# Attention and feed-forward block: x, attention's result and the output laid out by pairs and blocks of tiles in DRAM

## What is computed

```python
# cross attention: every query row sees 4 neighbouring rows of a table of 154 keys and values
q = split_heads(layernorm(x) @ Wq.T)                       # 16 heads of 32
k, v = split(ctx @ Wkv.T)
scores = einsum(q, k[seg_id - 0..3]) * 32 ** -0.5          # masked where the index is below 0
x = x + (softmax(scores) @ v[seg_id - 0..3]) @ Wo.T
# gated feed-forward, with every intermediate quantised to int16 by its own global peak
h = act_qdq(layernorm(x))
up, gate = act_qdq(h @ up_w.T), act_qdq(h @ gate_w.T)      # 4-bit weights, 1536 columns
gate = act_qdq(gate * fixed_qdq(sigmoid(gate)))
x = x + act_qdq(gate * up) @ down_w.T
```

## Time and profile before

| what | value |
|---|---|
| median of three runs | 2336.34 us |
| profiled execution, its own time | 2335.28 us |
| its span in the trace | 2333.4 us |
| PE, DVE, ACT, POOL busy | 87%, 76%, 58%, 29% of the span |
| DMA | 132025 packets, 637.74 MB, 273 GB/s |
| attention with its start and its drain | 0 to 642 us |
| products for gate and up | 646 to 1643 us |
| stretch without matmuls | 1643 to 1824 us |
| product for down, last stores | 1824 to 2333 us |

### The profile page before, as it was taken

How to read it: one execution, slowest core, us unless ns; L and a number is a source line. 1 busy time by engine, 2 the same in 40 slices (tenths; PEclk the granted TensorE clock), 3 DMA queues, 4 the chain that set the end, 5 groups by cost and what they waited for, 6 DMA issues and landing times.

```text
span 2333.4 us, 25335 instructions
## 1 busy us (share of the span) xinstructions
PE 2019.0 (87%) x9524; PEld 944.9 (40%) x9524; DVE 1766.4 (76%) x1404; ACT 1349.1 (58%) x1571; POOL 667.4 (29%) x664
## 2 busy tenths in 40 slices
PE   5888888888599999999999999999100799999998
PEld 2444444444344444444444444444000344444443
DVE  8799999999746756665599999999699744457541
ACT  4678788887422322222399886766699633446430
POOL 2599999999300000000011101222010000000000
PEclk9999999999899999999999999999655899999999
DMA  7789999998346755753699986886899855555641
GB/s 297 278 316 336 353 331 349 338 343 334 126 158 234 243 216 196 250 180 134 236 406 416 413 341 251 292 320 253 355 418 372 317 224 216 208 204 217 234 153 72
DMA packets 132025, 637.74 MB, mean 273 GB/s; under 512 B 12352, under 2 KB 12864, under 8 KB 91968
## 3 DMA queue, kind: packets, MB, share of 16 engines
q1 hardware_dynamic: 86464, 318.91, 37.4%
q0 software_dynamic: 45440, 317.21, 34.8%
HBM read 431.73 MB, written 204.34 MB: 273 GB/s over the span
## 4 chain that ended last, share of the span: by engine, by line
PE 64%; issue 2%; ACT 2%; DVE 2%; DMA 1%; POOL 0%; DVEq 0%; ACTq 0%; POOLq 0%
PE fd_pp L1810 43%; PE fd_pp L1824 21%; ACT ff_ring L1753 1%; DMA ff_ring<-gate_integers 1%; DVE ff_sig L1609 1%; DMA kept_gate<-gate_integers 0%; DVE ff_h_parts L1593 0%; ACT kept_gate L1757 0%; DVE ff_sq L1529 0%; ACT ff_gin L1757 0%; DVE ff_sq L1600 0%; ACT ff_hq L1757 0%; POOL ff_o_all L898 0%; ACT ff_sig L1740 0%; ACT ff_ring L1779 0%
## 5 line engine op out<-in xcount | busy, mean ns | idle before, releaser
L1824 PE MATMUL fd_pp<-ff_down,kept_gate 128*128 128x512 f16 x1536 | 458.3, 380 | 181.4 <-DVE ff_up L1650 181.4
L1810 PE MATMUL fd_pp<-ff_h_parts,kept_gate 128*128 128x512 f16 x2304 | 499.4, 380 | 14.2 <-DVE ff_h_parts L1421 14.2
L1810 PE MATMUL fd_pp<-ff_h_parts,ff_up 128*128 128x512 f16 x2304 | 497.4, 379 | 0.0
L1673 ACT ACTIVATE ff_raw<-fd_pp 128x1024 f32<-128x1024 f32 x192 | 195.1, 1020 | 399.5 <-PE fd_pp L1810 394.4
L1810 PEld LDWEIGHTS fd_pp<-ff_h_parts,kept_gate 128*128 128x128 f16 x2304 | 225.8, 98 | 287.7 <-DVE ff_h_parts L1421 14.6
L1810 PEld LDWEIGHTS fd_pp<-ff_h_parts,ff_up 128*128 128x128 f16 x2304 | 225.4, 98 | 271.9
L1824 PEld LDWEIGHTS fd_pp<-ff_down,kept_gate 128*128 128x128 f16 x1536 | 150.5, 98 | 363.7 <-issue 183.3
L1824 PE MATMUL fd_pp<-ff_down,ff_up 128*128 128x512 f16 x768 | 291.7, 380 | 0.0
L1437 DVE TENSOR_REDUCE ff_gate_top<-ff_raw 128x1 f32<-128x2048 f32 (+1 forms) x49 | 109.8, 2242 | 187.2 <-ACT ff_raw L1673 187.2
L1779 ACT ACTIVATE ff_ring<-ff_hq,kept_g 128x2048 int16<-128x2048 f32 x48 | 96.1, 2001 | 229.0 <-DVE ff_hq L1583 226.3
L790 PE MATMUL at_psO<-kept_wo,at_ahi 128*128 128x512 f16 x512 | 155.6, 386 | 36.2 <-ACT at_alo L277 31.6
(11 more groups left out here) (244 smaller groups left out, 3375.2 us busy)
## 6 DMA issues: line engine op xcount, KB each, us to landing
ff_raw<-up_scratch SPq DMA_DIRECT2D x66, 1024.0 KB, 8.4
gate_scratch<-ff_raw POOLq DMA_DIRECT2D x48, 1024.0 KB, 8.9
ff_gin<-gate_scratch SPq DMA_DIRECT2D x48, 1024.0 KB, 8.8
up_scratch<-ff_raw POOLq DMA_DIRECT2D x48, 1024.0 KB, 8.6
ff_gin<-gate_integers SPq DMA_DIRECT2D x77, 512.0 KB, 6.3
gate_integers<-ff_ring POOLq DMA_DIRECT2D x43, 512.0 KB, 11.5
ff_up<-up_scratch SPq DMA_DIRECT2D x21, 1024.0 KB, 8.8
kept_xs<-in_x SPq DMA_DIRECT2D x32, 512.0 KB, 14.6
```

Of the source, the lines that this page charges most:

```text
L1673: nc.scalar.activation(raw[:, n % UNITS, h * 2 * BLK:(h + 1) * 2 * BLK], pp[(2 * n + h) % 4][:, :, :].rearrange("p a t -> p (a t)"), ACT.C ...
L1810: mm = nc.tensor.matmul(pp[k % 4][:, h, :], wt[w][:, c, f:f + P], a[:, b % 2, :, c, :], start=(q == 0), stop=(q == len(todo) - 1))
L1824: mm = nc.tensor.matmul(pp[k % 8 // 2][:, k % 2, :], a[b % 2][:, f, t * P:(t + 1) * P], wt[w][:, f, :], start=(q == 0 and i == 0), stop=(q ...
```

## The change

The rows of x are put into another order on the host, so that in DRAM a pair is 128 pieces of 4 KB: partition p's row of the first tile and behind it its row of the second. `x1_scratch` and `hT_scratch` become tensors by block, partition and tile, so that a partition's four rows of a block lie together (8 KB). A pair's store writes half of each of these, 4 KB at a step of 8 KB; a block's load reads 8 KB per partition. The output is written in the same order by blocks, and the host turns it back. The buffers on the chip, the instructions of every engine, their order and their waits are the same as before: 398 rows of SP's list before and after, and the same number on the other engines. The last block's four stores are still 2 KB per partition, now at a step of 8 KB in DRAM.

```diff
-    x_v = x.rearrange("(n a p) d -> n p a d", p=P, a=2)
-    x1_v = x1_d.rearrange("(n a) p d -> n p a d", a=2)
-    hT_v = hT_d.rearrange("(n a) p d -> n p a d", a=2)
+    x_v = x.rearrange("(n p a) d -> n p a d", p=P, a=2)
...
-    hT_first = hT_d.rearrange("(b n) p d -> b p n d", n=SUB)
+
+    def half_block(t, p):
+        k = 2 * (p % 2)
+        return t[p // 2][:, k:k + 2, :]
...
-                        sp.dma_start(x1_v[p], xs[:, ring(p), :]).then_inc(x1_out[p % XR], 16)
+                        sp.dma_start(half_block(x1_d, p), xs[:, ring(p), :]).then_inc(x1_out[p % XR], 16)
...
-                        sp.dma_start(hT_v[p], hT[:, k:k + 2, :]).then_inc(hT_out[p % 2], 16)
+                        sp.dma_start(half_block(hT_d, p), hT[:, k:k + 2, :]).then_inc(hT_out[p % 2], 16)
...
-    out_v = out.rearrange("(b n p) d -> b p n d", p=P, n=SUB)
+    out_v = out.rearrange("(b p n) d -> b p n d", p=P, n=SUB)
...
-                        sp.dma_start(hb[b % 2].rearrange("p (n d) -> p n d", n=SUB), hT_v[b]).then_inc(h_in[b % 2], 16)
+                        sp.dma_start(hb[b % 2].rearrange("p (n d) -> p n d", n=SUB), hT_d[b]).then_inc(h_in[b % 2], 16)
...
-                        sp.dma_start(xb[:, b % 2], x1_v[b]).then_inc(x_in[b % 2], 16)
+                        sp.dma_start(xb[:, b % 2], x1_d[b]).then_inc(x_in[b % 2], 16)
...
-    x1_d = nc.dram_tensor("x1_scratch", [NT, P, D], F32).ap()
-    hT_d = nc.dram_tensor("hT_scratch", [NT, P, D], F32).ap()
+    x1_d = nc.dram_tensor("x1_scratch", [NB, P, SUB, D], F32).ap()
+    hT_d = nc.dram_tensor("hT_scratch", [NB, P, SUB, D], F32).ap()
```

More of the change, by code:

```diff
@@ L238, in _ @@
                             sp.wait_ge(hT_out[1], 16 * (b + 1))
-                            sp.dma_start(keep["h_first"][b].rearrange("p (n d) -> p n d", n=SUB), hT_first[b]).then_inc(h_in[b], 16)
+                            sp.dma_start(keep["h_first"][b].rearrange("p (n d) -> p n d", n=SUB), hT_d[b]).then_inc(h_in[b], 16)
                     if pair(p):
@@ L954, in feed @@
     FG, FU = 4, 3
-    hT_v = hT_d.rearrange("(b n) p d -> b p n d", n=SUB)
-    out_v = out.rearrange("(b n p) d -> b p n d", p=P, n=SUB)
-    x1_v = x1_d.rearrange("(b n) p d -> b p n d", n=SUB)
+    out_v = out.rearrange("(b p n) d -> b p n d", p=P, n=SUB)
     ready = [("kept", v) for v in (KEPT - 1, KEPT - 2, KEPT - 3)]
@@ L1896, in by_block, with rows_together @@
         return np.ascontiguousarray(w.reshape(w.shape[0], -1, QB).transpose(1, 0, 2)).reshape(P, -1)
+    def rows_together(a, n):
+        return np.ascontiguousarray(a.reshape(-1, n, P, D).transpose(0, 2, 1, 3)).reshape(-1, D)
     arrays = {
-        "x": np.ascontiguousarray(np.asarray(x).reshape(B * LQ, D)),
+        "x": rows_together(np.asarray(x).reshape(B * LQ, D), 2),
         "ctx_t": contraction_first(np.asarray(ctx_1024).reshape(B * LKV, D)),
@@ L1912 @@
     r = run_bass_kernel_spmd(nc, [{f"in_{n}": a for n, a in arrays.items()}], core_ids=[0])
-    return r.results[0]["out"].reshape(B, LQ, D)
+    by_block_out = r.results[0]["out"].reshape(-1, P, SUB, D)
+    return np.ascontiguousarray(by_block_out.transpose(0, 2, 1, 3)).reshape(B, LQ, D)
```

## The result

| | before | after |
|---|---|---|
| median | 2336.01 us (18 runs, 2334.04 to 2337.21) | 2339.86 us (18 runs, 2338.01 to 2341.22) |
| profiled execution, its span | 2333.4 us | 2338.2 us |
| packets | 132025 | 105529 |

The ratio is 1.0017, with a 95% interval of 1.0009 to 1.0024. It is under the 0.2% that I had called indistinguishable, but the interval lies wholly above 1: the change costs 2 to 6 us, and I had forecast no change.

The account below looks back on a forecast made before the run. The prediction took VectorE to bound the attention loop and TensorE the products; all terms were 0 but +0.1 us at the end, 2335.28 + 0.1 = 2335.4 us, forecast as 2336 us (median), range 2329.5 to 2341.

Parts of the forecast that it names:

- The bounds of the stages: TensorE bounds gate/up and down, VectorE (98.8 of 100 us) the attention loop; there no changed transfer is waited for.
- The removed packets: Whole kernel: larger pieces remove 30336 of 132025 packets, leaving about 101700, with the bytes the same.
- What a piece of 2 KB costs: Changed transfers: saving per byte between nothing and 8%; DMA share in the loop from 0.94 to 0.92 at best.
- Start, loop, feed: First loads of x, attention loop, gate/up/down products: terms 0 each; start bounded by -0.1 and +0.6 us.
- Drain of attention: End of attention: last hT store lands at 635.2, next part begins at 636.21; 1.0 us of cover, term 0.
- End: Last output stores, landing after 2.3 us, in 2 KB pieces 8 KB apart: +0.1 us, bounds 0 and +0.5.
- gain at a DMA limit: Attention loop follows the DMA engines and gets faster, at most about 6 us, to 2329 us; chance 0.14.
- slower stores with a step: Stores at a step of 8 KB are slower in DRAM; 2385 us if twice as long; chance 0.04.
- rows that don't merge: Whole kernel: pieces stay 2 KB and packets stay at 132025; time as forecast, 2336 us; chance 0.03.
- rival 2: Attention loop: gathers land later than their 23.8 us lead, so products wait; 2350 us; chance 0.05.

Follow-up runs that it names:

- e1: The kernel before with only the output's layout by blocks, x, x1 and hT as before; 2339.43 us, ratio 1.0016.
- e2: The changed kernel with the output back in its old layout, x, x1 and hT in the new one; 2335.30 us, ratio 0.9996.
- e3: The changed kernel with the last block's four output stores writing rows that lie together, as before; 2340.02 us, ratio 1.0019.
- e9: The changed kernel with 7 of the 15 output block stores as four tile stores each; 2336.86 us in one execution.
- e12: The changed kernel with three output block stores as eight stores of 128 KB each; 2337.91 us in one execution.
- e10: The changed kernel with 13 of the 15 output block stores as four tile stores each; 2337.35 us in one execution.
- e5: The changed kernel with all 15 output block stores issued as four tile stores each; 2339.68 us, ratio 1.0017.
- e6: The changed kernel with every output tile stored in two halves, 128 stores of 128 KB in all; 2332.04 us, ratio 0.9986.
- e4: The changed kernel with all 19 output stores moved from GpSimd's queue to SP's; 2330.99 us, ratio 0.9976.

## Why the prediction was wrong

**The bounds of the stages: right.** DVE bounds attention, TensorE the two products, and no changed transfer is waited for in any of them. That the other three layouts and 24576 packets moved the time by nothing measurable (ratio 0.9996) is this part of the prediction, tested alone.

**The removed packets: right on SP's queue, wrong on GpSimd's.** On SP's queue 86464 became 61888, exactly the 24576 of my count. On GpSimd's 45440 became 43520, 1920 fewer and not 15 x 384 = 5760: a block store of before already went in 256 packets of 4 KB in place of 512 of 2 KB. So 105529 are left and not 101700.

**What a piece of 2 KB costs: at the upper bound.** I had 0 to 8% between the gathers' 43.2 engine-us per MB and 39.4 from the stretch without matmuls; it is 39.7, 8% less. The 28 later loads of x land after 11.5 us in place of 14.3. In the loop the DMA share goes from 0.94 to 0.92 by it, and no time comes of it: DVE, busy 98.8 of 100 us, covers it.

**Start, loop, feed: zero, as forecast.** Gathers land in 11.9 us, at most 17.5, against 11.7 and 17.4, so that no product waits. The 0.54 us by which the changed kernel's profile is later at DVE's first product may be chance or the layout's. The three traces with the old loads of x are there at 59.7 to 60.5 us, the eleven with the new ones at 60.0 to 61.6. These overlap, executions of the kernel before spread by 3 us (2334.04 to 2337.21), and the ratio of 0.9996 with all new layouts but the output's shows no loss; a few tenths of a us stay open.

**Drain of attention: zero, for another reason (here the part of the prediction called Drain, not the instruction).** I held that the next part starts when the last hT store has landed and DVE is through, at 636.21, and gave that store 1.0 us of cover. In fact GpSimd's DRAIN at the end of opening, 6.55 us from 633.9, ends at 640.4, and all the others wait for it. The store, landed at 635.2, had 5 us of cover. The next row of the timeline should have warned me: nothing that I had named explains the gap from 636.2 to 641.9 us.

**End: this step failed.** I wrote: "The last store is issued at 2324.26; the last ones land after 2.3 us. It keeps its 2 KB pieces, now 8 KB apart. Bounds: 0, and +0.5 us". The term measures +4.0 us. The landing of the last store, 2326.6 us, is not the end of the span, 2333.4; 6.8 us lie between, a time larger than everything that I was weighing, and I never asked what fills it. GpSimd's DRAIN takes 5.12 us of them, and 9.13 us after the change, because its length depends on the earlier stores from GpSimd, whose form the change alters (9.13 us with the output's layout alone, e1, and 5.12 with all but it, e2). The step that failed is to take the last landing for the end; no bound from landings could hold this. Once these 6.8 us had been seen, the trace of before would have shown the DRAIN, its place on the path and a second one in opening. That the output's form would lengthen it and not shorten it, no row of before tells; a DRAIN anywhere between 0 and twice its 5.12 us would have been an honest bound.

**The rivals.** None of the four is what happened: no gain at a DMA limit (ratio 0.9996 without the output's layout), no late gather, no slower stores with a step (those of the last block land after 2.3 us with it and without it, those of x1 after 14.2 us in the median in place of 14.5, those of hT after 9.4 in place of 9.6), no rows that don't merge (105529 packets). For rival 2's 24.0 to 25 us of landing, its time of 2350 us and its 0.05 no run shows a source: the gathers landed after 11.9 us in the median and 17.5 at most, where they had 11.7 and 17.4, against the 23.8 us of lead. The range, to 2341 us, holds the time only by luck: it was opened that far for late gathers, and they did not come.

## What to carry to other kernels

Account for the whole span: name what fills the time between the last landing and the last instruction, and between two parts of a program, also where no engine is busy. Here GpSimd's DMAs had a closing cost (1.37 to 9.29 us) that depended on the number and form of all of them and not on the last one alone; with the last stores on GpSimd it lay open at the end, and giving them to SP hid it (ratio 0.9975, the old layouts kept). Larger pieces in DRAM lowered the DMA share from 0.94 to 0.92 here, under an engine that was busy 98.8%, and so paid nothing; what they pay where DMA is the bound, no run here shows.

## What the runs showed of the hardware

- GpSimd's DRAIN at the end of the kernel takes 1.37 to 9.29 us by the number and form of its DMAs, and the same number of ns in kernels whose DMAs are alike (9126 ns in after, e1 and e3, 5124 in before and e2). DVE's closing one takes 0.783 to 0.785 us in all fourteen.
- Where GpSimd still had an operation to run, the length shown for the DRAIN contains the time until that was done: 11.02 us with the stores on SP, of which 8.66 after the operation; 6.33 to 6.81 us at the end of opening, of which 5.32 after it, or 5.57 with three more DMAs.
- It isn't the time of GpSimd's transfers: at the end of the kernel before it begins at 2326.7 us, when the last store has landed (2326.5 us), and with the stores on SP at 1817.7 us, 27 us after GpSimd's last DMA was issued. It grew by 0.0817 us for each DMA more between 240 (before), 261 (e9, e12), 279 (e10) and 285 (e5), and yet more DMAs came with a shorter one: 64 stores gave 8.80 us (e5), 128 gave 1.37 (e6).
- GpSimd issues a store of 1 MB in pieces of 2 KB in 752 ns (median of 15, before), the same store in pieces of 8 KB in 531 ns (after).
- GpSimd's queue had fewer packets than pieces of 2 KB: it had 46160 with all stores by tile (e5) and 41040 with none (e4), 5120 for 64 stores, 80 for each store of 128 pieces, though these lie 8 KB apart in DRAM. Of the 80, 16 are under 512 B (13072 of these in e5 in place of 12352 after, with 45 stores more), which leaves 64 of 4 KB. SP's queue lost 24576 packets (86464 to 61888), which is 256 - 128 for each of 96 pairs and 512 - 128 for each of 32 blocks, so there each piece of 2 KB had been a packet.
